# An attention stage whose inverse goes through memory: L is sent out before its diagonal is set, and four steps change their place

## The chip, the cores and the metric

One Trainium2 chip, one core of it. The metric is the device time of one execution in microseconds (us). TensorE does matmuls and 128x128 transposes, DVE is VectorE, ACT is ScalarE, POOL is GpSimd, SP is SyncE, which here only issues DMAs.

## The reference, cut to what matters

The program runs four layers on x of 32 x 256 tokens of 128 features, each with a layer norm before it and a residual after it: attention, feed-forward, a state-space layer, feed-forward. The change is in attention, a gated delta rule:

```
q, k, v = x@Wq+bq, x@Wk+bk, x@Wv+bv
k = k / max(norm(k), 1e-12)
alpha, beta, gate = sigmoid(x@Wa+ba), sigmoid(x@Wb+bb), sigmoid(x@Wg+bg)
for each token t:                      # S is 128 x 128 for each of the 32 sequences
    S = S @ (alpha_t * (I - beta_t * k_t k_t^T)) + beta_t * v_t k_t^T
    o_t = (q_t @ S) * gate_t
y = o @ Wo + bo
```

## The kernel before, in words

The kernel computes attention in blocks of 128 tokens ("tiles"). Four tiles, two whole sequences, are a group; there are 16 groups. In a tile the sequential rule becomes a triangular system: with L the matrix of gated products of keys (unit diagonal), the kernel needs the inverse of L and applies it to v. A sequence is two tiles, so the second tile's v is first corrected by what the first tile wrote.

The inverse is built bottom up. Its 16x16 diagonal blocks ("leaves", eight in a tile, 32 in a group) are brought to 32 partitions by writing L to memory (`LT_dram`) and reading back only the leaves (`leafV`). GpSimd eliminates them in 14 pairs of small operations (`leaf_steps`, L571 and L575), DVE makes 2I - V of them (`leafR`, L1136), and they go out (`R_dram`) and back as a block-diagonal matrix `Rm`. From there the levels 16, 32 and 64 are joined on TensorE (`times_M`, `times_T`), with transposes by DVE and copies by ACT between them.

The order of the work is written out by hand. `in_order` calls, on each engine, `attention_half` (on SP `leaves_half`) for h = 0 to 18, with up to four groups in flight: b = group h (k projection, norm of k, decay, L), s = h - 1 (leaves), i = h - 2 (v, the rest of the inverse, q, gate), e = h - 3 (applying the inverse, outputs), and nxt, whose layer norm is being made. Every engine runs its instructions in the order of the code; semaphores join the engines. `wait_ge(X, done(n))` waits until X has been done for group n.

What each engine does in a half, as far as the change and the working speak of it:
- TensorE: k (L1560), w0 (L1568: inverse times v for the first tile of each of the two sequences), v (L1575), spread alpha (L1582), correction (L1591), Z4 (L1542), WT (L1603: for all four tiles v transposed times R), T4 (L1549), transposes of k (L1613), PT (L1621), Z5 (L1542), G (L1634), transposes of x (L1536), O (L1645, L1647), T5 (L1549), q (L1656), Z6, y (L1666), gate (L1671), R6.
- DVE: bias of k (L1071), shift of the layer norm (L1028), `Tm` by transposing `Rm` (L1081), bias of v (L1084), sum of k's squares (L1089) and its maximum with 1e-24 (L1091), v's correction (L1096), the mask of level 16 (L1046), normalised k (L1106), scans (L1112), the gate on PT and later on L (L1056, twice), leafR (L1136), og = O times gate (L1143), transposes of level 32 (L1149), the residual (L1155).
- GpSimd: bias onto x (L584), rstd of the layer norm (L555, L558), leaf steps 1 to 3, 1/norm of k (`kinv`, L594), leaf steps 4 to 14, and last the select that sets L's diagonal to one (L600).
- ACT: sigmoid, copies out of PSUM, k's squares (L785).
- SP: R's leaves out (L496), L out (L500), R in (L506), L's leaves in (L511). A wait of SP is recorded one line above the issue that stands behind it.

Of the kernel before, what the change touches and what calls it, by code (L numbers as in the profile page):

```python
# [75 lines left out]
def build(nc, x_in, Wq, bq, Wk, bk, Wv, bv, Wa, ba, Wb, bb, Wg, bg, Wo, bo,  # L76
# [7 lines left out]
    with ctx:  # L84
# [208 lines left out]
        LEAF_STEPS = 2 * (LEAF - 2)  # L293
# [5 lines left out]
        def done(n):  # L299

            return n + STREAMS + 1
# [126 lines left out]
        def _(sp):  # L428
# [62 lines left out]
            def leaves_half(b, s, i, e, nxt):  # L491

                if s is not None:
                    n, k = s
                    sp.wait_ge(leaf_done, done(n))
                    sp.dma_start(dram_leaves(R_dram[k % 2]), leaf_grid(leafR[k % 2][:, :])).then_inc(R_out, 16)  # L496
                if b is not None:
                    n, k = b
                    sp.wait_ge(LT_done, done(n))
                    sp.dma_start(dram_tiles(LT_dram[k % 2]), tile4(LT[k][:, 0:GROUP])).then_inc(LT_out, 16)  # L500
# [6 lines left out]
                if b is not None:  # L507
                    n, k = b
                    sp.wait_ge(LT_out, landed(n))
                    sp.wait_ge(leaf_done, done(n - 2))  # L510
                    sp.dma_start(leaf_grid(leafV[k % 2][:, :]), dram_leaves(LT_dram[k % 2])).then_inc(leaf_in, 16)  # L511
# [33 lines left out]
        def _(pool):  # L545
# [14 lines left out]
            def leaf_steps(n, k, first, last):  # L560

                V = leaf_grid(leafV[k % 2][:, :])
                for s in range(first, last):
                    below = LEAF - 1 - s
                    prod = leaf_tmp[:, 0:s * below].rearrange("r (c t) -> r c t", t=below)
                    at = LEAF_STEPS * n + 2 * (s - 1)
                    if s == 1:
                        pool.wait_ge(leaf_in, landed(n))
                    if at > 0:
                        pool.wait_ge(leaf_step, at)  # L570
# [7 lines left out]
            def attention_half(b, s, i, e, nxt):  # L578

                if e is not None:  # L580
# [16 lines left out]
                if b is not None:  # L597
                    n, k = b
                    pool.wait_ge(LTraw_done, done(n))
                    nc.gpsimd.affine_select(out=tile4(LT[k][:, 0:GROUP]), in_=tile4(LT[k][:, 0:GROUP]),  # L600
                                            compare_op=ALU.not_equal, fill=1.0, base=0,
                                            pattern=[[0, GROUP_TILES], [-1, P]], channel_multiplier=1).then_inc(LT_done, 1)
# [406 lines left out]
        def _(dve):  # L1009
# [51 lines left out]
            def attention_half(b, s, i, e, nxt):  # L1061
# [15 lines left out]
                if i is not None:  # L1077
# [4 lines left out]
                    dve.wait_ge(v_mm, done(n))  # L1082
                    dve.wait_ge(WT_mm, done(n - 2))
                    nc.vector.tensor_tensor(tile4(vtok[k % 2]), tile4(begin_bank[2][:, :]), per_tile(bv_row[:, :]),  # L1084
                                            ALU.add).then_inc(v_done, 1)
                if b is not None:
# [4 lines left out]
                    nc.vector.tensor_scalar(kss[k % 2], kss[k % 2], 1e-24, None, ALU.max).then_inc(kmax_done, 1)  # L1091
                if e is not None:
# [894 lines left out]
```

## Time and profile before

| | us |
|---|---|
| median of 3 runs | 880.91 (879.55 to 883.13) |
| the profiled execution | 879.69 |
| its span, first to last instruction | 877.9 |
| TensorE busy, share of the span | 773.3, 88% |
| DVE busy | 621.8, 71% |
| GpSimd busy | 561.6, 64% |
| ACT busy | 535.7, 61% |

The span is what the traces divide; the time lies 1.8 us above it. Busy time is no bound by itself: an engine that is 88% busy over the span may be filled in one stage and wait in another. The attention stage ends at about 346 us; the rest of the span belongs to the three later layers.

### The profile page before, as it was taken

The page shows a single profiled execution, that of the slowest core. Times are in us where ns is not written, and L with a number is a line of the kernel's source. Part 1 is how long each engine was busy: PE and PEld are TensorE (multiplying, and loading weights), DVE is VectorE, ACT ScalarE, POOL GpSimd, SP SyncE. Part 2 cuts the span into 40 slices and gives each one's busy share as a digit, 9 for nine tenths or more (in the row PEclk, how much of TensorE's full clock was granted, in tenths as well). Part 3 has the DMA queues.
Part 4 walks back from the last instruction along what each step waited for, and adds up shares of the span by engine and source line. Part 5 has one row for each costly group of instructions (what it writes and reads, how often), then busy time and mean ns, then how long its engine had stood idle before and what let it go on. Part 6 is the DMA issues. An engine that isn't in the chain of part 4 may idle for free. (4 is left out here: it accounts for less than half of the span.)

```text
span 877.9 us, 16088 instructions
## 1 busy us (share of the span) xinstructions
PE 773.3 (88%) x5146; PEld 551.7 (63%) x5146; DVE 621.8 (71%) x1739; ACT 535.7 (61%) x1035; POOL 561.6 (64%) x901
## 2 busy tenths in 40 slices
PE   1369999999999895999856999999999999959997
PEld 1258888888888774666634456656555555545665
DVE  1357878777878753888664678888887777637885
ACT  2224443443345323888644878978887788828986
POOL 1267567666766620788711579778868876757785
PEclk9979999999999999999955899999999999979999
DMA  7511111111111100000000000000000000000112
GB/s 195 134 28 37 46 28 28 38 46 28 28 42 41 29 14 1 1 1 0 2 0 8 1 1 3 7 1 2 9 0 1 7 4 1 1 0 25 48 49 73
DMA packets 59420, 22.16 MB, mean 25 GB/s; under 512 B 22224, under 2 KB 59088, under 8 KB 59344
## 3 DMA queue, kind: packets, MB, share of 16 engines
q1 hardware_dynamic: 59344, 21.23, 9.5%
q8 instruction: 37, 0.61, 0.3%
q14 instruction: 39, 0.32, 0.1%
HBM read 11.59 MB, written 9.63 MB: 24 GB/s over the span
## 5 line engine op out<-in xcount | busy, mean ns | idle before, releaser
L1405 DVE SCALAR_TENSOR_TENSOR arena<-bank,convw_sb,arena 128x510 f32<-128x510 f32 (+2 forms) x192 | 142.4, 744 | 42.2 <-ACT arena L898 37.5
L667 POOL TENSOR_TENSOR arena<-arena 128x768 f32<-128x768 f32 x64 | 114.9, 1815 | 12.8 <-ACT arena L925 10.9
L641 POOL TENSOR_TENSOR arena<-ff,arena 128x512 f16<-128x512 f32 x64 | 73.6, 1159 | 23.0 <-ACT arena L867 21.0
L571 POOL TENSOR_TENSOR leaf_tmp<-leafV 32x14 f32<-32x14 f32 (+6 forms) x224 | 55.8, 249 | 37.1 <-DMA leafV<-LT_dram 21.8
L862 ACT ACTIVATE ff<-bank 128x512 f32<-128x512 f32 x96 | 56.2, 586 | 32.2 <-PE bank L1708 32.0
L770 ACT ACTIVATE ff<-bank 128x256 f32<-128x256 f32 (+2 forms) x80 | 33.9, 424 | 65.1 <-PE bank L1549 37.7
L575 POOL TENSOR_TENSOR leafV<-leafV,leaf_tmp 32x14 f32<-32x14 f32 (+6 forms) x224 | 62.3, 278 | 17.6
L1795 PE MATMUL bank<-xnT,win_sb 128*128 128x512 f32 x128 | 71.8, 645 | 0.0
L1221 DVE SCALAR_TENSOR_TENSOR ff<-bank,ff 128x512 f32<-128x512 f32 x96 | 64.6, 684 | 8.9 <-ACT ff L862 8.0
L919 ACT ACTIVATE arena<-bank 128x384 f32<-128x384 f32 x128 | 59.8, 492 | 15.5 <-PE bank L1810 15.3
L755 ACT ACTIVATE xnT<-bank 128x512 f32<-128x512 f32 x34 | 20.3, 596 | 79.1 <-PE bank L1536 79.0
L763 ACT ACTIVATE xn<-x_all,shift,rstd 128x128 f32<-128x128 f32 x136 | 55.6, 480 | 18.8 <-DVE shift L1028 18.8
L555 POOL TENSOR_TENSOR var_eps<-mv,eps_cols 128x4 f32<-128x4 f32 x34 | 7.1, 210 | 93.0 <-DVE mv L1021 93.0
L1056 DVE SCALAR_TENSOR_TENSOR arena<-bank,arena 128x256 f32<-128x256 f32 (+1 forms) x128 | 44.6, 411 | 24.1 <-PE bank L1621 16.2
L673 POOL TENSOR_TENSOR arena<-arena 128x512 f32<-128x512 f32 x32 | 40.1, 1268 | 29.8 <-DVE arena L1412 29.4
L898 ACT ACTIVATE arena<-bank,convb_sb,convw_sb 128x512 f32<-128x512 f32 x64 | 49.9, 781 | 11.9 <-PE bank L1795 11.9
L1821 PE MATMUL bank<-arena 128*64 128x256 f32 (+1 forms) x512 | 48.4, 332 | 3.5 <-DVE x_all L1277 2.6
L1536 PE MATMUL bank<-tab,xn 128*128 128x128 f32 x136 | 24.0, 306 | 28.5 <-issue 16.5
L1821 PEld LDWEIGHTS bank<-arena 128*64 128x64 f32 x512 | 31.9, 136 | 25.7 <-issue 11.7
L1707 PE MATMUL bank<-xh,gate 128*128 128x512 f16 x96 | 37.7, 393 | 8.6 <-DVE xl L1206 7.9
L1808 PE MATMUL bank<-ff 12*128 12x384 f16 x128 | 43.1, 337 | 2.3 <-ACT arena L919 2.3
L1808 PEld LDWEIGHTS bank<-ff 12*128 12x128 f16 x128 | 11.6, 91 | 52.4 <-issue 25.1
(199 smaller groups left out, 2239.2 us busy)
## 6 DMA issues: line engine op xcount, KB each, us to landing
LT_dram<-arena SPq DMA_DIRECT2D x16, 256.0 KB, 2.4
ff<-R_dram SPq DMA_DIRECT2D x16, 256.0 KB, 3.0
out<-x_all SPq DMA_DIRECT2D x8, 512.0 KB, 3.2
x_all<-in_L_attn_a_x SPq DMA_DIRECT2D x7, 512.0 KB, 7.3
ff<-pieces_dram SPq DMA_DIRECT2D x48, 6.0 KB
x_all<-in_L_attn_a_x SPq DMA_DIRECT2D x2, 256.0 KB, 3.6
R_dram<-tab SPq DMA_DIRECT2D x2, 256.0 KB, 2.7
leafV<-LT_dram SPq DMA_DIRECT2D x16, 32.0 KB, 2.7
```

Of the source, the lines that this page charges most:

```text
L571: nc.gpsimd.tensor_tensor(prod, V[:, s:s + 1, s + 1:LEAF].broadcast_to([leaf_rows, s, below]), V[:, 0:s, s:s + 1].broadcast_to([leaf_rows, ...
L575: nc.gpsimd.tensor_tensor(V[:, 0:s, s + 1:LEAF], V[:, 0:s, s + 1:LEAF], prod, ALU.subtract).then_inc(leaf_step, 1)
L641: nc.gpsimd.tensor_tensor(of_block(hl[u], j), hidT[u][:, j, :], of_block(hh[u], j), ALU.subtract).then_inc(hl_done[u], 1)
L667: nc.gpsimd.tensor_tensor(score[h], cb[g % 2], hgam[h], ALU.mult).then_inc(score_done, 1)
L763: last = nc.scalar.activation(xn[u][:, cols(t)], x_all[:, n % GROUPS * GROUP + t * P:n % GROUPS * GROUP + (t + 1) * P], ACT.Identity, scal ...
L862: nc.scalar.activation(silu_g[u][:, j, :], bank[u][(1, 3, 1)[j]][:, :], ACT.Silu, scale=DEQUANT).then_inc(silu_done[u], 1)
L919: nc.scalar.activation(hgam[h][:, batch * TRI:(batch + 1) * TRI], step_bank[batch][:, 0:TRI], ACT.Exp).then_inc(hgam_done, 1)
L1221: nc.vector.scalar_tensor_tensor(hidT[u][:, j, :], bank[u][(2, 0, 2)[j]][:, :], DEQUANT, silu_g[u][:, j, :], ALU.mult, ALU.mult).then_inc( ...
L1405: nc.vector.scalar_tensor_tensor(acc_of[:, :, s:SEQ], src_of[:, :, 0:SEQ - s], convw_sb[:, r, TAPS - 1 - s:TAPS - s], acc_of[:, :, s:SEQ], ...
L1795: mm(conv_bank[r % 2][:, :], win_sb[:, INNER + r * P:INNER + (r + 1) * P], xnT[b % XNT_SETS][:, :], start=True, stop=True).then_inc(conv_m ...
L1808: mm(to[:, 0:TRI], from_rows[side][rows, at * P:(at + 1) * P], to_rows[side][rows, at * TRI:(at + 1) * TRI], start=True, stop=False)
L1821: last = mm(y_bank[r][k * HEAD_DIM:(k + 1) * HEAD_DIM, batch * SEQ + c * P:(batch + 1) * SEQ], x_of[:, 2 * batch + c, h * HEAD_DIM:(h + 1) ...
```

## The change

- L is written to memory as soon as DVE has gated it (`LTraw_done`), with whatever stands on its diagonal. SP issues it first in its half, ahead of R's leaves; the leaves' read comes before R's read.
- The leaves' diagonals are set to one by a memset of `leafV` ahead of the first leaf step; the leaf steps wait for the select as well. A group's leaf work counts 29 steps instead of 28.
- The select on L itself moves from the end of GpSimd's half, for b, to the start of the next one, for the same group (now s). It waits until L's copy out has landed.
- On DVE, the sum of k's squares and the maximum move ahead of v's bias; the two parts of v (bias, correction) now follow one another. og moves ahead of leafR.
- On TensorE, WT of the first tile of each sequence is made by transposing `w0tok` (the same values, since w0 is R transposed times v), before the wait for the corrected v; two tiles of matmuls are left behind that wait.

```diff
-        LEAF_STEPS = 2 * (LEAF - 2)
+        LEAF_STEPS = 2 * (LEAF - 2) + 1
...
+                if b is not None:
+                    n, k = b
+                    sp.wait_ge(LTraw_done, done(n))
+                    sp.dma_start(dram_tiles(LT_dram[k % 2]), tile4(LT[k][:, 0:GROUP])).then_inc(LT_out, 16)
                 if s is not None:
                     n, k = s
                     sp.wait_ge(leaf_done, done(n))
                     sp.dma_start(dram_leaves(R_dram[k % 2]), leaf_grid(leafR[k % 2][:, :])).then_inc(R_out, 16)
                 if b is not None:
                     n, k = b
-                    sp.wait_ge(LT_done, done(n))
-                    sp.dma_start(dram_tiles(LT_dram[k % 2]), tile4(LT[k][:, 0:GROUP])).then_inc(LT_out, 16)
+                    sp.wait_ge(LT_out, landed(n))
+                    sp.wait_ge(leaf_done, done(n - 2))
+                    sp.dma_start(leaf_grid(leafV[k % 2][:, :]), dram_leaves(LT_dram[k % 2])).then_inc(leaf_in, 16)
                 if s is not None:
                     n, k = s
                     sp.wait_ge(WT_mm, done(n - 2))
                     sp.wait_ge(T_done, done(n - 2))
                     sp.wait_ge(R_out, landed(n))
                     sp.dma_start(tile4(Rm[k % 2]), dram_tiles(R_dram[k % 2])).then_inc(R_in, 16)
-                if b is not None:
-                    n, k = b
-                    sp.wait_ge(LT_out, landed(n))
-                    sp.wait_ge(leaf_done, done(n - 2))
-                    sp.dma_start(leaf_grid(leafV[k % 2][:, :]), dram_leaves(LT_dram[k % 2])).then_inc(leaf_in, 16)
...
-                    at = LEAF_STEPS * n + 2 * (s - 1)
+                    at = LEAF_STEPS * n + 2 * (s - 1) + 1
                     if s == 1:
                         pool.wait_ge(leaf_in, landed(n))
-                    if at > 0:
-                        pool.wait_ge(leaf_step, at)
+                        pool.wait_ge(LT_done, done(n))
+                        if n > 0:
+                            pool.wait_ge(leaf_step, at - 1)
+                        nc.gpsimd.memset(leafV[k % 2][:, 0:LEAF * LEAF:LEAF + 1], 1.0).then_inc(leaf_step, 1)
+                    pool.wait_ge(leaf_step, at)
...
+                if s is not None:
+                    n, k = s
+                    pool.wait_ge(LTraw_done, done(n))
+                    pool.wait_ge(LT_out, landed(n))
+                    nc.gpsimd.affine_select(out=tile4(LT[k][:, 0:GROUP]), in_=tile4(LT[k][:, 0:GROUP]),
+                                            compare_op=ALU.not_equal, fill=1.0, base=0,
+                                            pattern=[[0, GROUP_TILES], [-1, P]], channel_multiplier=1).then_inc(LT_done, 1)
                 if e is not None:
...
                 if s is not None:
                     leaf_steps(*s, 4, LEAF - 1)
-                if b is not None:
-                    n, k = b
-                    pool.wait_ge(LTraw_done, done(n))
-                    nc.gpsimd.affine_select(out=tile4(LT[k][:, 0:GROUP]), in_=tile4(LT[k][:, 0:GROUP]),
-                                            compare_op=ALU.not_equal, fill=1.0, base=0,
-                                            pattern=[[0, GROUP_TILES], [-1, P]], channel_multiplier=1).then_inc(LT_done, 1)
...
                     nc.vector.transpose(Tm[k % 2], Rm[k % 2]).then_inc(T_done, 1)
-                    dve.wait_ge(v_mm, done(n))
-                    dve.wait_ge(WT_mm, done(n - 2))
-                    nc.vector.tensor_tensor(tile4(vtok[k % 2]), tile4(begin_bank[2][:, :]), per_tile(bv_row[:, :]),
-                                            ALU.add).then_inc(v_done, 1)
                 if b is not None:
                     n, k = b
                     dve.wait_ge(ksq_done, done(n))
                     nc.vector.tensor_reduce(kss[k % 2], tile4(ksq[k % 2]), AX.X, ALU.add).then_inc(kss_done, 1)
                     dve.wait_ge(kss_done, done(n))
                     nc.vector.tensor_scalar(kss[k % 2], kss[k % 2], 1e-24, None, ALU.max).then_inc(kmax_done, 1)
+                if i is not None:
+                    n, k = i
+                    dve.wait_ge(v_mm, done(n))
+                    dve.wait_ge(WT_mm, done(n - 2))
+                    nc.vector.tensor_tensor(tile4(vtok[k % 2]), tile4(begin_bank[2][:, :]), per_tile(bv_row[:, :]),
+                                            ALU.add).then_inc(v_done, 1)
...
+                if e is not None:
+                    n, k = e
+                    dve.wait_ge(OT_mm, done(n))
+                    dve.wait_ge(g_done, done(n))
+                    dve.wait_ge(y_mm, done(n - 2))
+                    nc.vector.tensor_tensor(og[k % 2], end_bank[2][:, :], gT[k % 2], ALU.mult).then_inc(og_done, 1)
                 if s is not None:
                     n, k = s
                     dve.wait_ge(leaf_step, LEAF_STEPS * (n + 1))
                     V, eye2 = leaf_grid(leafV[k % 2][:, :]), leaf_grid(two_eye)
                     nc.vector.scalar_tensor_tensor(leaf_grid(leafR[k % 2][:, :]), V, -1.0, eye2,
                                                    ALU.mult, ALU.add).then_inc(leaf_done, 1)
-                if e is not None:
-                    n, k = e
-                    dve.wait_ge(OT_mm, done(n))
-                    dve.wait_ge(g_done, done(n))
-                    dve.wait_ge(y_mm, done(n - 2))
-                    nc.vector.tensor_tensor(og[k % 2], end_bank[2][:, :], gT[k % 2], ALU.mult).then_inc(og_done, 1)
...
                     n, k = e
+                    pe.wait_ge(og_done, done(n - 1))
+                    for t in range(BATCHES):
+                        nc.tensor.transpose(end_bank[2][:, cols(2 * t)], w0tok[k % 2][:, cols(t)], ident)
                     pe.wait_ge(v1_done, done(n))
-                    pe.wait_ge(og_done, done(n - 1))
-                    for t in range(GROUP_TILES):
+                    for t in range(1, GROUP_TILES, 2):
                         last = mm(end_bank[2][:, cols(t)], vtok[k % 2][:, cols(t)], Rm[k % 2][:, cols(t)], start=True, stop=True)
                     last.then_inc(WT_mm, 1)
```

## Rows read from the trace of the kernel before

**Rows 1.** Windows: length; busy of PE, PEld, DVE, ACT, POOL; granted clock; DMA.
```profile
71.98:281.01 209.03, 202.74 (x1538) 176.51 (x1537) 163.80 (x475) 89.02 (x194) 138.52 (x395) 1.00 0.15 35
246.87:263.94 17.07, 16.76 (x131) 14.66 (x129) 13.65 (x41) 7.33 (x17) 11.61 (x33) 1.00 0.16 39
```

**Rows 2.** Waits from 60 to 320 us: waiter, releaser, us, times, longest.
```profile
POOL leaf_tmp L571 <- DMA leafV<-LT_dram: 11.4, 11, 2.0
...
SPq L505 <- DMA R_dram<-leafR: 16.4, 15, 2.6
```

**Rows 3.** Timeline of TensorE's matmuls in the quiet half: start, us, operation, count.
```profile
250.09 1.00 PE L1542 MATMUL bank<-ff,arena 128*128 128x64 f32 x8
251.40 1.16 PE L1603 MATMUL bank<-ff,arena 128*128 128x128 f32 x8 [0.31 <-DVE arena L1096]
252.39 1.00 PE L1549 MATMUL bank<-ff 128*128 128x64 f32 x8
253.23 0.60 PE L1613 MATMUL bank<-tab,arena 128*128 128x128 f32 x4
253.67 1.47 PE L1621 MATMUL bank<-arena,ff 128*128 128x256 f32 x8
```

**Rows 4.** Timeline of DVE in the same half.
```profile
248.94 0.70 DVE L1081 STREAM_TRANSPOSE ff<-ff 128x512 f32<-128x512 f32 x1
249.57 0.65 DVE L1084 TENSOR_TENSOR arena<-bank,bv_row 128x512 f32<-128x512 f32 x1
250.15 0.67 DVE L1089 TENSOR_REDUCE arena<-arena 128x4 f32<-128x512 f32 x1
...
250.93 0.41 DVE L1096 TENSOR_TENSOR arena<-arena,bank 128x256 f32<-128x256 f32 x1
...
252.14 0.74 DVE L1106 TENSOR_TENSOR arena<-arena 128x512 f32<-128x512 f32 x1 [0.47 <-POOL arena L594]
...
257.44 1.39 DVE L1056 SCALAR_TENSOR_TENSOR arena<-bank,arena 128x256 f32<-128x256 f32 x4
259.81 0.83 DVE L1136 SCALAR_TENSOR_TENSOR leafR<-leafV,tab 32x256 f32<-32x256 f32 x1 [0.98 <-POOL leafV L575]
```

**Rows 5.** Timeline of ACT in the same half.
```profile
248.99 0.63 ACT L785 ACTIVATE arena<-arena 128x512 f32<-128x512 f32 x1
```

**Rows 6.** Timeline of GpSimd in the same half.
```profile
247.75 1.02 POOL L558 TENSOR_TENSOR rstd<-var_eps,half_neg 128x4 f32<-128x4 f32 x1
249.08 0.20 POOL L571 TENSOR_TENSOR leaf_tmp<-leafV 32x14 f32<-32x14 f32 x1 [0.31 <-DMA leafV<-LT_dram]
...
251.10 1.01 POOL L594 TENSOR_TENSOR arena<-arena,half_neg 128x4 f32<-128x4 f32 x1 [0.28 <-DVE arena L1091]
...
259.74 0.63 POOL L600 TENSOR_SCALAR_AFFINE_SELECT arena<-arena 128x512 f32<-128x512 f32 x1
260.35 1.45 POOL L584 TENSOR_TENSOR arena<-x_all,bo_row 128x512 f32<-128x512 f32 x1
```

**Rows 7.** Timeline of SP's issues in the same half: start of issue, us.
```profile
260.67 0.32 SPq L496 DMA_DIRECT2D R_dram<-leafR  x1
261.04 0.48 SPq L500 DMA_DIRECT2D LT_dram<-arena  x1
262.46 0.38 SPq L506 DMA_DIRECT2D ff<-R_dram  x1
263.46 0.32 SPq L511 DMA_DIRECT2D leafV<-LT_dram  x1
```

**Rows 8.** A memset on GpSimd at the start of the program: ns min/median/max.
```profile
L546 POOL MEMSET half_neg<- x1: 104/104/104, 0.7 to 0.7; 128x8 f32 x1
```

**Rows 9.** Timeline of DVE from 68 to 70 us.
```profile
68.77 0.40 DVE L1136 SCALAR_TENSOR_TENSOR leafR<-leafV,tab 32x256 f32<-32x256 f32 x1
```

**Rows 10.** Timeline of DVE from 57 to 60 us, in the third half.
```profile
57.69 0.71 DVE L1081 STREAM_TRANSPOSE ff<-ff 128x512 f32<-128x512 f32 x1 [2.77 <-DMA ff<-R_dram]
```

**Rows 11.** The page's list of DMA issues: KB each, median us from issue to landing.
```profile
ff<-R_dram SPq DMA_DIRECT2D x16, 256.0 KB, 3.0
```

## The prediction

> **What bounds the kernel now.** I read the windows first, the attention stage as a whole and one half of it, then the waits, then the timelines of one half of the attention stage engine by engine. The change touches the attention stage alone. There the kernel runs nineteen "halves" (16 groups and a lag of 3); a half works on group b at its start, s (select and leaf inverse), i (the rest of the inverse) and e (outputs). Twelve full halves, from the k projection of one at 71.98 us to that of another at 281.01 us, take 209.03 us, and TensorE is busy in 202.74 of them with the full 2.4 GHz granted (1.00); a single quiet half takes 17.07 us with TensorE busy for 16.76 [rows 1]. Twelve quiet ones would be 204.84, so 4.19 us in this stretch are something else than the usual pace.
>
> The usual pace is TensorE's. The one place where it stands in a quiet half is before L1603 (WT = v times R): 0.31 us recorded as idle, for the corrected v of DVE's L1096 [rows 3, 4]. From start to start it is more: L1542's eight matmuls take 0.84 (the spacing of L1549 to L1613, which is the same shape: 252.39 to 253.23), so TensorE could go on at 250.09 + 0.84 = 250.93 and goes on at 251.40, 0.47 lost.
>
> The 4.19 us come from the second loop, which runs over GpSimd and SP: leaf steps end (GpSimd), select L600, leafR on DVE, R out, L out after it, L's leaves back in, leaf steps again. In the quiet half it closes with hardly any slack: leaf steps end just ahead of 259.74, L's copy out is issued at 261.04, the leaves' read at 263.46 [rows 6, 7], and L571 has already waited for such a read 11 times for 11.4 us in all, up to 2.0 [rows 2]. R's own copy out also landed late sometimes: L505 waited 16.4 us over 15 times, a mean of 1.09, but up to 2.6 [rows 2]. When either transfer is late by about one us, the half lasts longer.
>
> **L out without its diagonal.** Now L goes out when DVE's L1056 ends, 257.44 + 1.39 = 258.83 [rows 4], not after leaf steps, select and R's issue at 261.04 [rows 7]: 2.2 us earlier. Its leaves are then read 2.42 us after its issue (261.04 to 263.46), as now, so the whole L to leaf path starts 2.2 us earlier. GpSimd does not gain that: it first must do rstd, whose 1.02 us end at 248.77, and the first leaf step begins at 249.08 [rows 6], so 0.31 is what it can gain. A memset of the leaf diagonals is added there. Nearest row: a memset of 128x8 takes 0.104 [rows 8]; with the 0.08 that a dependent GpSimd operation follows behind its predecessor's end, 0.18; the upper bound is the start-to-start step of a leaf operation, 0.28 (1.74, below, over six), the lower 0.10. With 0.18 the steps start at 248.98 at the latest, about 0.1 earlier than now, and the price is covered. After three pairs of steps (249.08 to 251.10, less about 0.28 idle, 1.74) GpSimd is ready for kinv at 250.72.
>
> **Select at the head of the half.** L600 (0.63) leaves the end of the leaf steps and moves to where GpSimd sat waiting for mv. It waits for L's landing, 258.5 + 2.42 = 260.9 (the times from here on already have the 0.4 us of the sum taken off), so it ends at 261.6, and the bias add of 1.45 behind it ends at 263.0; rstd of the next half starts at 247.75 [rows 6] + 17.07 - 0.4 = 264.4, with a small addition of 0.3 ahead of it, so GpSimd is wanted at 264.1. Slack 1.1 us. Queued behind this wait are the bias add, rstd and all leaf steps; DVE's shift, and with it the whole chain to v, waits for rstd. Cost nothing while L lands within 3.5 us of its issue.
>
> **leafR.** It took 0.83 while select ran on GpSimd (259.74) [rows 4, 6], and 0.40 when GpSimd was not selecting [rows 9]. Now select has not begun, so I take 0.40. The Trainium skill says of this ("SBUF — State Buffer", who interferes with whom) that a vector instruction with two SBUF inputs and a GpSimd one that reads SBUF exclude each other for the whole instruction; the two rows agree. With the steps' end at 259.4 (kinv is 0.38 earlier, see below), leafR ends at 259.85 and R goes out at 259.9, not 260.67; R in follows 1.79 later (260.67 to 262.46 [rows 7]) at 261.7 and, landing 3.0 after its issue [rows 11], is there at 264.7. DVE wants it at 248.94 + 17.07 - 0.4 = 265.6 [rows 4]: slack 0.9, where it was 0.55. SP's order changes too: the leaves' read now stands ahead of R in. It is issued at 260.9, before R in may be, and delays it by nothing. og ahead of leafR: og needs the O matmuls only and uses DVE's 0.98 us idle before leafR [rows 4]; its consumer L1666 stands behind q and Z6 on TensorE, so this is worth nothing in a quiet half, and something in those where the leaf steps end late.
>
> **Squares of k ahead of v's bias and correction.** DVE runs T (L1081), bias add (L1084), reduce (L1089), max, correction (L1096). With the reduce moved up, it would start at 249.57, where the bias add starts; but the squares end on ScalarE at 248.99 + 0.63 = 249.62 [rows 5], 249.65 with the semaphore. So the corrected v comes 0.08 later, the rest of the sum being the same operations. Reduce and max take 0.78 up to the next operation (250.15 to 250.93 [rows 4]), so kmax comes at about 249.65 + 0.8 = 250.5; GpSimd is ready at 250.72, kinv starts then, 0.38 earlier than 251.10 [rows 6]. kn follows 1.04 later at 251.76 instead of 252.14 and ends at 252.5 [rows 4]; the transposes of kn on TensorE (253.23, or 252.8 after the gain below) never wait for it: cover 0.3 us, which a memset of 0.28 would still leave at 0.2.
>
> **Two transposes ahead of the corrected v.** For the even tiles WT is the transpose of w0, which is in SBUF already. Four transposes take 0.44 from start to start (L1613, 253.23 to 253.67), eight instructions of four matmuls 0.99 (L1603 to L1549) [rows 3]. So 0.50 of matmuls leave the path behind the wait and 0.22 of transposes go into the 0.47 of the wait. New start of T4: 251.40 + 0.08 + 0.50 = 251.98 instead of 252.39, a gain of 0.41; if the first pair pays its start alone (half of the 0.99 is then 0.55), 0.36. I take 0.40. Everything behind it (T4, kT, PT, Z5, G, O, T5, q, Z6, y, g, R6) runs without a gap on TensorE and moves up by it, since the waits there (copies on ScalarE, gates on DVE) all follow from TensorE's own results.
> The Trainium skill ("TensorE: Matmul & The Clock Gate", Part 4: PE-mode transpose) says that transposes do not count as busy for the clock as matmuls do. That speaks against trading matmuls for transposes. The twelve halves had twelve transposes each (L1582, L1613, L1536) and were granted 1.00 throughout [rows 1]; two more in each is what is new.
>
> **The sum.** Thirteen full halves (the twelve and the next) by 0.40: 5.2. Of the 4.19 us of late transfers, those of the leaves' read vanish (landed by 263.4, wanted at 265.4 when rstd ends: 2 us of slack); a late R can still cost, with 0.9 of slack: I leave 1.0, so 3.2 gained. The last three halves: the last one has no other group's work between the steps of its one group, so TensorE waits for v there and half of the 0.99 is saved, the other two save some 0.28 each: 1.0. The first halves: T of the first inverse waited 2.77 us for R's read behind L's copy out, until 57.69 [rows 10]; L now leaves before it, and I take that wait to be about 0.9 shorter, against 0.3 for a select and memset that stand ahead of the first kinv: 0.6. Total 10.0 us. The profiled execution took 879.69 with a span of 877.9, so 869.7 in its like; the median of the three runs is 880.91, which gives 870.9. I say 871.0. What follows the stage (both feed-forward stages and the state-space stage) is untouched.
>
> **Rivals.** About 4.4 us, half a per cent, is what a measurement can tell from none.
> *The forecast*, 60 in 100: 868 to 873.
> *Late transfers stay or find another victim* (R out and R in instead of the leaves), 18 in 100: the gain is 5.2 + 1.0 + 0.6, so 874. For it: the longest wait of L505 was 2.6 against a mean of 1.09, more than the slack of 0.9. Against it: most of the late ones were the leaves'.
> *TensorE packs wholly*, 7 in 100: if v came early enough to hide the wait, a half would lose 0.47 + 0.28 = 0.75, 13 of them 9.8, and the time would be 866. Against it: nothing in v's chain gets shorter.
> *Nothing comes of it*, 8 in 100: squares later than thought (a slip of 0.5 instead of 0.08 eats the transposes' gain) and the late transfers stay: 879.
> *Slower*, 5 in 100: select waits for L's landing at the head of GpSimd's queue. It decides from a landing 3.5 us after issue; to be 4.4 us slower than now it must be 14.4 / 13 = 1.1 us beyond that in each half, 4.6 us after issue, where 2.42 is seen: 886.
> *The clock gate*, 2 in 100: TensorE is busy for 16.76 us of a half at 2.4 GHz [rows 1]; one half wholly at 1.2 GHz would cost up to 16 us and bring 887. By the skill's rule this could follow from the transposes; the granted 1.00 speaks against it.
> The range 866 to 876 leaves out the last three cases and a little more. Faster by over half a per cent 0.85, within 0.09, slower 0.06.
>
> **What the profile after would show.** From one k projection to the next 16.7 us in quiet halves. Two transposes of w0 start right behind Z4, and TensorE's wait for v stands between them and four matmuls. No wait of the leaf product for its read; leafR at 0.40, og before it. kinv 0.4 us earlier against T. The forecast is wrong if the wait for v grows beyond 0.25, if T waits for R's read, or if var_eps waits for GpSimd itself.

## The result, and the profile after

The changed kernel takes 868.59 us, median of four executions (867.31 to 870.12), against 880.62 for the kernel before on the same chip: a ratio of 0.9865, with a 95% interval from 0.9835 to 0.9894. The profiled execution took 869.76 with a span of 868.0, 9.9 less than before's 877.9. (Ratios and their intervals here and below are worked out from the single executions, so a ratio can differ a little from the quotient of two medians.)

The windows answer to [rows 1]: the same twelve halves, and one quiet half.

```profile
71.18:272.84 201.66, 198.84 (x1514) 172.30 (x1513) 158.49 (x475) 89.14 (x194) 139.74 (x410) 1.00 0.15 37
239.31:256.07 16.76, 16.55 (x128) 14.36 (x126) 13.22 (x41) 7.33 (x17) 11.53 (x34) 1.00 0.15 38
```

The twelve take 7.37 us less. A quiet half takes 16.76 instead of 17.07, and eleven of the twelve are quiet (before: five within 0.06 of the quiet length, the others up to 18.33). The columns are those of [rows 1]; the granted clock, 1.00, is unchanged.

TensorE in a quiet half, from its timeline (start, us, operation, count, idle before):

```profile
242.53 1.00 PE L1548 MATMUL bank<-ff,arena 128*128 128x64 f32 x8
243.37 0.39 PE L1608 MATMUL bank<-tab,arena 128*128 128x128 f32 x2
243.97 0.71 PE L1611 MATMUL bank<-ff,arena 128*128 128x128 f32 x4 [0.21 <-DVE arena L1102]
244.52 1.00 PE L1555 MATMUL bank<-ff 128*128 128x64 f32 x8
245.36 0.61 PE L1621 MATMUL bank<-tab,arena 128*128 128x128 f32 x4
```

The two transposes (L1608) stand where TensorE stood idle in [rows 3]. Two tiles of matmuls are left behind the wait for v (L1611), and T4 (L1555) follows 0.55 after they start, not 0.99.

DVE in the same half (it answers to [rows 4]):

```profile
241.39 0.70 DVE L1085 STREAM_TRANSPOSE ff<-ff 128x512 f32<-128x512 f32 x1
242.10 0.69 DVE L1089 TENSOR_REDUCE arena<-arena 128x4 f32<-128x512 f32 x1
242.82 0.17 DVE L1091 TENSOR_SCALAR arena<-arena 128x4 f32<-128x4 f32 x1
242.90 0.69 DVE L1096 TENSOR_TENSOR arena<-bank,bv_row 128x512 f32<-128x512 f32 x1
243.51 0.41 DVE L1102 TENSOR_TENSOR arena<-arena,bank 128x256 f32<-128x256 f32 x1
243.84 0.42 DVE L1050 TENSOR_TENSOR ff<-bank,tab 128x256 f32<-128x256 f32 x1
244.17 0.68 DVE L1112 TENSOR_TENSOR arena<-arena 128x512 f32<-128x512 f32 x1
...
247.32 1.39 DVE L1060 SCALAR_TENSOR_TENSOR arena<-bank,arena 128x256 f32<-128x256 f32 x4 [0.66 <-PE bank L1629]
...
251.27 0.69 DVE L1143 TENSOR_TENSOR arena<-bank,arena 128x512 f32<-128x512 f32 x1 [0.30 <-PE bank L1655]
251.88 0.40 DVE L1148 SCALAR_TENSOR_TENSOR leafR<-leafV,tab 32x256 f32<-32x256 f32 x1
```

From T to v's correction are 2.12 us (241.39 to 243.51), where before they were 1.99: the reduce starts 0.08 later than DVE could, as worked out, and 0.05 more goes into the order of the rest. Normalised k (L1112) starts without a wait. leafR takes 0.40.

GpSimd and SP around the end of the half (they answer to [rows 6, 7]):

```profile
243.07 1.01 POOL L604 TENSOR_TENSOR arena<-arena,half_neg 128x4 f32<-128x4 f32 x1
...
253.48 0.64 POOL L587 TENSOR_SCALAR_AFFINE_SELECT arena<-arena 128x512 f32<-128x512 f32 x1 [1.72 <-DMA LT_dram<-arena]
254.09 1.28 POOL L594 TENSOR_TENSOR arena<-x_all,bo_row 128x512 f32<-128x512 f32 x1
256.68 0.20 POOL L555 TENSOR_TENSOR var_eps<-mv,eps_cols 128x4 f32<-128x4 f32 x1 [1.32 <-DVE mv L1025]
```

SP's instructions, from the timeline of its queue:

```profile
251.00 0.38 SPq L496 DMA_DIRECT2D LT_dram<-arena  x1
252.31 0.32 SPq L500 DMA_DIRECT2D R_dram<-leafR  x1
253.30 0.32 SPq L505 DMA_DIRECT2D leafV<-LT_dram  x1
254.09 0.38 SPq L511 DMA_DIRECT2D ff<-R_dram  x1
```

L goes out first, select waits for it on an engine that has nothing else to do, and after the bias add GpSimd is still idle for 1.3 us before var_eps: this is the slack that the prediction put at 1.1. No leaf product and no var_eps waits for a DMA in any quiet half. The leaves' read, which now stands ahead of R's, also takes less itself: a median of 1.9 us from issue to landing, where it was 2.7.

Where the 9.9 us went, from the starts of the k projection and of the residual add in both traces: the first three halves 0.80, the twelve full halves 7.37, from there to the thirteenth residual add 0.33, and the last three halves took 0.65 more than before (49.60 against 48.95). The stage ends 7.85 us earlier. From the start of the last residual add to the end of the span 530.15 us pass, where they were 532.2, 2.05 less in this pair of executions. The code there is the same, and in the twelve other profiles below this part takes 529.2 to 535.8 us, so these 2 us are not put down to the change.

### The profile page after: what moved, and what is told of

It is laid out like the page before. It is cut to its first block and busy times, and to the rows that moved or that the text cites. A ratio compares the mean times of both kernels' runs of the same rounds, so it can differ in the third digit from the quotient of the medians.

```text
span 868.0 us, 16041 instructions
## 1 busy us (share of the span) xinstructions
PE 769.9 (89%) x5114; PEld 549.0 (63%) x5114; DVE 614.7 (71%) x1739; ACT 535.9 (62%) x1035; POOL 560.6 (65%) x917
```

## The experiments

All are made from the kernel before or from the changed kernel. The length of a quiet half is read from one k projection to the next. A ratio compares with the kernel before on the same chip; its median there was 882.74 us for the path of L, the two transposes and the two orders on DVE, 880.79 for v's bias, the reductions, both and the changed kernel again, and 881.23 for the rest. The expectations start from 880.9 or 868.6.

**The path of L alone.** The kernel before with the changes on SP and GpSimd, without those on DVE and TensorE; the read of the leaves is issued ahead of that of R, too.

```diff
@@ leaves_half, SP @@
+                if b is not None:
+                    n, k = b
+                    sp.wait_ge(LTraw_done, done(n))
+                    sp.dma_start(dram_tiles(LT_dram[k % 2]), tile4(LT[k][:, 0:GROUP])).then_inc(LT_out, 16)
                 if s is not None:
...
@@ leaf_steps, GpSimd @@
+                        nc.gpsimd.memset(leafV[k % 2][:, 0:LEAF * LEAF:LEAF + 1], 1.0).then_inc(leaf_step, 1)
...
@@ attention_half, GpSimd @@
+                if s is not None:
+                    n, k = s
+                    pool.wait_ge(LTraw_done, done(n))
+                    pool.wait_ge(LT_out, landed(n))
+                    nc.gpsimd.affine_select(out=tile4(LT[k][:, 0:GROUP]), in_=tile4(LT[k][:, 0:GROUP]),
...
```

> The kernel before with the path of L alone (L out before its diagonal, select at the head of GpSimd's half, memset of the leaves' diagonals, SP's order); DVE's order and TensorE's four tiles of WT matmuls are those of before. Theory (two loops): the quiet half stays at 17.07 us, since TensorE's wait for v is untouched, and the longer halves (17.3 to 18.3) vanish, so about 3.7 us from these, 0.7 from the first halves: 876. Rival (the path of L is hidden anyway, the gain of the changed kernel is all TensorE's): 880 to 881, with halves of 17.6 still there.

Measured: ratio 0.9948 (0.992 to 0.9976), median 878.16: 4.6 us gained, about what had been expected. The quiet half is 17.07, as it should be. No leaf product waits for its read in a full half any more. But four of the twelve halves are long (17.93, 17.61, 17.53, 18.5), not none. The profiled execution, 885.46 us, is the longest of the twelve executions, so it does not stand for all. In each of the four halves DVE's T waits for the read of R, in the longest like this:

```profile
196.23 0.71 DVE L1085 STREAM_TRANSPOSE ff<-ff 128x512 f32<-128x512 f32 x1 [1.33 <-DMA ff<-R_dram]
```

and the list of DMAs of the window 189 to 193 us shows what was under way:

```profile
q8 instruction: 1, 0.02, 2.2%
q14 instruction: 1, 0.01, 0.8%
issues: line engine op xcount, KB each, median us to landing
ff<-R_dram SPq DMA_DIRECT2D x1, 256.0 KB, 3.4
R_dram<-leafR SPq DMA_DIRECT2D x1, 32.0 KB, 3.6
leafV<-LT_dram SPq DMA_DIRECT2D x1, 32.0 KB, 2.9
```

R's leaves out took 3.6 us instead of the usual 1.7, in a window in which the instruction queues loaded two pieces. In the halves of 17.61 and 17.53 the copy out took 1.7, but R's read 4.45 and 4.41 instead of 2.8. The path of L is worth something alone (half a per cent), for the leaves; it does not keep R from being late, so the expectation's "the longer halves vanish" was too much.

**The two transposes alone**, made in the kernel before.

```diff
@@ attention_half, TensorE @@
+                    pe.wait_ge(og_done, done(n - 1))
+                    for t in range(BATCHES):
+                        nc.tensor.transpose(end_bank[2][:, cols(2 * t)], w0tok[k % 2][:, cols(t)], ident)
                     pe.wait_ge(v1_done, done(n))
-                    pe.wait_ge(og_done, done(n - 1))
-                    for t in range(GROUP_TILES):
+                    for t in range(1, GROUP_TILES, 2):
```

> The kernel before with the two transposes of w0 in WT alone. Theory (two loops): TensorE alone could do a half in 17.07 - 0.44 = 16.63, but the loop of leaf steps, select, L out and leaves in takes 17.07 less its 0.28 us idle at kinv, 16.8, and now has no slack against a late transfer: quiet halves of 16.8 at best, late ones as long as before, 877 to 879. Rival (the parts add up): 13 halves by 0.44 and 0.8 at the end, 874.

Measured: ratio 0.9986 (0.9953 to 1.0019), median 881.22: no difference that can be told, and by the medians 1.5 us gained where 2 to 4 had been expected. TensorE's side works, T4 starts 0.55 after L1605; and what was gained is lost three lines on, at the transposes of k, which wait for DVE's normalised k:

```profile
93.98 0.71 PE L1605 MATMUL bank<-ff,arena 128*128 128x128 f32 x4
94.53 1.00 PE L1549 MATMUL bank<-ff 128*128 128x64 f32 x8
96.03 0.66 PE L1615 MATMUL bank<-tab,arena 128*128 128x128 f32 x4 [0.50 <-DVE arena L1106]
```

Behind this stands GpSimd, whose leaf steps began late:

```profile
92.49 0.20 POOL L571 TENSOR_TENSOR leaf_tmp<-leafV 32x14 f32<-32x14 f32 x1 [1.13 <-DMA leafV<-LT_dram]
```

The halves of this execution (884.95 us, above the median) are 17.0 to 17.7, and one 20.06, in which T waits 1.70 for R. In ten of the twelve the leaf product waits over 0.8 us for its read. The second loop, over leaves and memory, has become the bound. The theory of two loops holds, more strongly than expected: it gave 16.8 for the best halves, and only 16.98 was seen.

**Everything but the transposes**: the diff above, the other way round, in the changed kernel.

```diff
@@ attention_half, TensorE @@
-                    for t in range(BATCHES):
-                        nc.tensor.transpose(end_bank[2][:, cols(2 * t)], w0tok[k % 2][:, cols(t)], ident)
                     pe.wait_ge(v1_done, done(n))
-                    for t in range(1, GROUP_TILES, 2):
+                    pe.wait_ge(og_done, done(n - 1))
+                    for t in range(GROUP_TILES):
```

> The changed kernel with the WT of all four tiles by matmuls behind the corrected v, as before. Theory: the 0.44 us of two tiles of matmuls come back on the path behind v, which is 0.13 later than in the kernel before, so a quiet half takes 17.2 us, 0.44 more than 16.76, thirteen of them 5.7 and 0.8 at the end: 875. Rival (the transposes only fill a wait that another releaser ends anyway, the gain is the earlier L): 16.8 to 16.9, 870.

Measured: ratio 0.9959 (0.9931 to 0.9987), median 877.95; the quiet half is 17.20, as expected:

```profile
248.52 1.00 PE L1548 MATMUL bank<-ff,arena 128*128 128x64 f32 x8
249.96 1.16 PE L1609 MATMUL bank<-ff,arena 128*128 128x128 f32 x8 [0.43 <-DVE arena L1102]
250.95 1.00 PE L1555 MATMUL bank<-ff 128*128 128x64 f32 x8
```

0.44 us a half are the transposes', 0.13 of them pay for the later v. The time is 3 us above the expected 875. In the profiled execution 1.7 us of it are two halves (18.2 and 17.93) in which T waits 1.03 and 0.76 for R. So the transposes alone give 0.1%, which is not told from nothing, the rest without them 0.4%, both together 1.35%: the two parts give more together than the sum of what each gives alone.

**The two orders on DVE put back**, each alone in the changed kernel. First v's bias (L1096) back ahead of the squares of k:

```diff
                     nc.vector.transpose(Tm[k % 2], Rm[k % 2]).then_inc(T_done, 1)
+                    dve.wait_ge(v_mm, done(n))
+                    dve.wait_ge(WT_mm, done(n - 2))
+                    nc.vector.tensor_tensor(tile4(vtok[k % 2]), tile4(begin_bank[2][:, :]), per_tile(bv_row[:, :]),
+                                            ALU.add).then_inc(v_done, 1)
                 if b is not None:
```

Then leafR (L1148) back ahead of og:

```diff
                     gated(LT_strip, LT[k], k, begin_bank).then_inc(LTraw_done, 1)
-                if e is not None:
-                    n, k = e
-                    dve.wait_ge(OT_mm, done(n))
-                    dve.wait_ge(g_done, done(n))
-                    dve.wait_ge(y_mm, done(n - 2))
-                    nc.vector.tensor_tensor(og[k % 2], end_bank[2][:, :], gT[k % 2], ALU.mult).then_inc(og_done, 1)
                 if s is not None:
...
```

> The changed kernel with v's bias ahead of k's squares again. Theory: v is corrected 0.13 us earlier, but kinv starts 0.45 later and the transposes of k then wait some 0.07 for kn, so a half of 16.70 instead of 16.76 and 0.8 us less in all: within 1.5 us of the changed kernel's 868.6. Rival (the squares' place is what lets kn and TensorE be in time): kinv 0.4 later costs 0.3 us or more a half, 873 or above.

> The changed kernel with og behind leafR again. Theory: og ends by 252.97 where TensorE asks for it at 253.52, leafR and R out come 0.1 us earlier, nothing else moves: 868.6, the half 16.76. Rival (og's place is part of the gain): y waits, half longer by 0.2 or more, 871.

Measured: 0.9885 (0.9837 to 0.9932) with the squares back, 0.9881 (0.9835 to 0.9926) with og back; the changed kernel's 0.986 lies in both intervals. The quiet half is 16.83 with the squares back and 16.76 with og back. In the first, what the earlier v gives is taken by the transposes of k, which wait for kn at 245.42 (0.15 behind the end of T4's eight): the order is worth 0.07 us a half, where 0.06 the other way had been expected. og's place is worth nothing in a quiet half, as expected; the times, 875.13 and 873.62 in the median, are too scattered to say more. The single executions of both spread from 868 to 876 us. The profiled one with the squares back shows one reason. Its last half took 18.36 us, that of the changed kernel 14.22. The windows of both follow, first with the squares back (length, busy shares as above, then the granted clock):

```profile
324.90:343.50 18.60, 13.47 (x60) 10.28 (x58) 3.65 (x10) 6.58 (x13) 0.00 (x0) 0.67 0.00 0
```

The changed kernel's:

```profile
323.60:337.90 14.30, 9.13 (x58) 6.87 (x57) 3.69 (x10) 6.58 (x13) 0.00 (x0) 1.00 0.00 1
```

In one the granted clock is 0.67 on average, in the other 1.00, with the same work. TensorE stands idle there six times between short pieces, since one group alone is left.

**v's bias out of v's way.** The bias add is for group i, the correction behind it for group e. Nothing ties them, so the add goes behind the scans, ahead of the gate on PT.

```diff
                     nc.vector.tensor_scalar(kss[k % 2], kss[k % 2], 1e-24, None, ALU.max).then_inc(kmax_done, 1)
-                if i is not None:
-                    n, k = i
-                    dve.wait_ge(v_mm, done(n))
-                    dve.wait_ge(WT_mm, done(n - 2))
-                    nc.vector.tensor_tensor(tile4(vtok[k % 2]), tile4(begin_bank[2][:, :]), per_tile(bv_row[:, :]),
-                                            ALU.add).then_inc(v_done, 1)
...
                     last.then_inc(gam_done, 1)
+                if i is not None:
+                    n, k = i
+                    dve.wait_ge(v_mm, done(n))
+                    dve.wait_ge(WT_mm, done(n - 2))
+                    nc.vector.tensor_tensor(tile4(vtok[k % 2]), tile4(begin_bank[2][:, :]), per_tile(bv_row[:, :]),
+                                            ALU.add).then_inc(v_done, 1)
```

> The changed kernel with v's bias (0.69 us on DVE) moved from in front of the correction to behind the scans, where DVE is idle for 0.66 us; the bias is for another group than the correction. Theory (v's chain on DVE is the last limit): the corrected v is there 0.6 us earlier, ahead of the end of the two transposes, TensorE packs, a half takes about 16.4 (16.76 less the 0.38 from 243.59 to 243.97), thirteen of them 5 us: 864. Rival (the next limit is right behind, kn or T waiting for R's read, or GpSimd): half 16.65 or more, 867 to 868.

Measured: ratio 0.9809 (0.9765 to 0.9853), median 863.02, 5.5 less than the changed kernel on the same chip (868.48). The intervals of the two ratios still overlap a little; the halves tell the difference. Eleven of the twelve halves take 16.39, and TensorE goes from the transposes to the matmuls without a wait:

```profile
240.12 0.39 PE L1608 MATMUL bank<-tab,arena 128*128 128x128 f32 x2
240.34 0.61 PE L1611 MATMUL bank<-ff,arena 128*128 128x128 f32 x4
240.80 1.10 PE L1555 MATMUL bank<-ff 128*128 128x64 f32 x8
```

while DVE does the bias where it was idle before PT's gate:

```profile
239.65 0.41 DVE L1096 TENSOR_TENSOR arena<-arena,bank 128x256 f32<-128x256 f32 x1
...
243.34 0.66 DVE L1120 TENSOR_TENSOR arena<-bank,bv_row 128x512 f32<-128x512 f32 x1
243.92 1.38 DVE L1060 SCALAR_TENSOR_TENSOR arena<-bank,arena 128x256 f32<-128x256 f32 x4
```

v's chain on DVE was the last limit of the changed kernel's half. At 16.39 TensorE is busy for the whole of it.

**The reductions of the weights one half later.**

```diff
-                if h == GROUPS:
+                if h == GROUPS + 1:
                     all_weights = ff_raw[:, :, :].rearrange("p k h -> p (k h)")
```

> The changed kernel with the two reductions over the feed-forward weights (2.7 us on DVE) one half later. In their half TensorE waits 2.92 us for T, and its clock is then granted at 0.6 to 0.7 for some 7 us. Theory (the 1.4 us that this half became longer with the change are the clock after that wait): the wait shrinks to about 0.5, the clock stays at the higher level, and the half loses 2.5 to 5 us: 864 to 866. Rival (that half is bound by leaf steps or R's copy): under 1 us, 868.

Measured: ratio 0.9838 (0.9797 to 0.9879), median 866.6, which by the intervals is not told from the changed kernel; the profile tells it. The half takes 15.17, TensorE's wait for T is 0.19 instead of 2.92, and the clock of the first 15 us is granted in full. In the changed kernel's first profile this half took 21.06 with 0.77 granted; in its repetition on this chip, below, 17.88 with 1.00. So 2.7 us are the wait's; the other 3.2 of the 21.06 went with the clock, and they were gone in the repetition without this edit. The windows, first with the reductions late:

```profile
290.00:305.00 15.00, 13.69 (x103) 11.54 (x102) 8.95 (x25) 6.04 (x13) 10.14 (x33) 1.00 0.08 20
```

The changed kernel's:

```profile
289.50:304.50 15.00, 10.97 (x62) 10.15 (x61) 7.49 (x23) 3.60 (x9) 9.29 (x32) 0.77 0.03 8
```

Part of it is given back in the two halves behind (15.13 and 15.58 against 14.32 and 14.22). The reductions, which now stand in the first of them, are hardly the reason: behind them T still waits 0.32 for R's read, and the repetition below, with the reductions in their old place, has 15.01 and 15.58. In the last half the eight matmuls of PT (L1629) took 2.93 us instead of 1.57, with 0.89 granted over the half.

**Both.**

The two diffs above together, in the changed kernel.

> Both of the two before. Theory: they touch different halves and add up, 860 to 861. Rival: one eats the other, 864.

Measured: ratio 0.9777 (0.9735 to 0.9819), median 859.83 (857.67 to 866.0), 8.6 less than the changed kernel on the same chip. The two gains add up, as expected, and this version beats both kernels.

**The changed kernel again**, as the base of that chip.

> The changed kernel itself, for a base on the same chip: 868.6, halves of 16.76 us.

Measured: 868.48 (867.15 to 870.25), ratio 0.986 (0.9824 to 0.9896). Ten of the twelve halves take 16.76, the first 17.31 and the last 17.32. In the last, T waits for R, whose read took 4.7 us instead of 2.8:

```profile
257.92 0.71 DVE L1085 STREAM_TRANSPOSE ff<-ff 128x512 f32<-128x512 f32 x1 [0.60 <-DMA ff<-R_dram]
```

The half with the weights' reductions took 17.88 us here, with the same wait of 2.9 and the clock granted at 1.00 behind it; the last two took 15.01 and 15.58. So the 21.06 of the first execution are not in the code. Of the twelve profiles with the reductions in this place, two have 17.9 in this half and ten have 19.4 to 22.0.

**The price and the cover of the memset**: 3 more of them, and in the second kernel 8, on a tile that nothing reads.

```diff
+        spare = sb("spare", [leaf_rows, 8 * LEAF])
...
+                        for more in range(3):
+                            nc.gpsimd.memset(spare[:, more * LEAF:(more + 1) * LEAF], 1.0)
                         nc.gpsimd.memset(leafV[k % 2][:, 0:LEAF * LEAF:LEAF + 1], 1.0).then_inc(leaf_step, 1)
```

> The changed kernel with three memsets of 32x16 more (into a spare tile) ahead of the leaves' own, 0.12 us each by its trace. Theory: kinv comes 0.28 to 0.36 later, kn ends 0.5 ahead of TensorE's need for it, so the half stays at 16.76. Rival (GpSimd bounds the half as well): the half grows by the 0.36.

> The same with eight more memsets, some 0.9 us. Theory: kinv 0.85 later is 0.3 to 0.4 more than the cover of 0.5, so the half grows to 17.1 or 17.2: this is the point from which a memset would have cost. Rival (nothing waits for kinv that long): 16.76.

Measured, one execution each: 867.89 and 872.39 us, the quiet half 16.76 and 16.75. The longer time of the second is not in its quiet halves; its last half took 18.32, the one with the reductions 20.89. Eight memsets that nothing waits for took 0.42 us together, not 0.9:

```profile
240.51 0.42 POOL L574 MEMSET spare<- 32x16 f32 x8
240.87 0.12 POOL L575 MEMSET leafV<- 32x16 f32 x1
```

DVE at normalised k in the same half:

```profile
243.80 0.75 DVE L1115 TENSOR_TENSOR arena<-arena 128x512 f32<-128x512 f32 x1 [0.22 <-POOL arena L607]
```

DVE now waits 0.22 for kinv, and TensorE does not notice. The memset costs nothing, and 0.36 more would not either; where the cover ends was not reached.

**SP's order**: the read of R ahead of the read of the leaves again.

```diff
-                if b is not None:
-                    n, k = b
-                    sp.wait_ge(LT_out, landed(n))
-                    sp.wait_ge(leaf_done, done(n - 2))
-                    sp.dma_start(leaf_grid(leafV[k % 2][:, :]), dram_leaves(LT_dram[k % 2])).then_inc(leaf_in, 16)
                 if s is not None:
...
                     sp.dma_start(tile4(Rm[k % 2]), dram_tiles(R_dram[k % 2])).then_inc(R_in, 16)
+                if b is not None:
+                    n, k = b
+                    sp.wait_ge(LT_out, landed(n))
+                    sp.wait_ge(leaf_done, done(n - 2))
+                    sp.dma_start(leaf_grid(leafV[k % 2][:, :]), dram_leaves(LT_dram[k % 2])).then_inc(leaf_in, 16)
```

> The changed kernel with SP issuing the read of R ahead of the read of the leaves, as before. Theory (a late R is the work of packets of the instruction queues on one DMA ring, wherever SP's order stands): halves of 16.76, R asked for 1.79 us behind its own copy out, leaves 0.9 later and still in time, at most the odd late half. Rival (the leaves' read in front delays R): T no longer waits at all and the odd long halves are gone; or the leaves are late and the half is over 16.9 throughout.

Measured, one execution: 871.14 us. The halves are 16.76 but for the first and one of 17.83, in which GpSimd's memset waited 1.44 us for the leaves and TensorE 0.87 at the transposes of k. The read of the leaves is issued 0.46 behind that of R (239.10 and 239.56), 3.6 us after L's copy out instead of 2.3, and takes a median of 2.6 us instead of 1.9; in the long half it took 4.4. With SP's old order the leaves can be late again; SP's order is part of what keeps them off the path. One half in one execution shows how it can go, not how often.

## Why the prediction was right

**TensorE's wait for v is the pace of a quiet half: right, the size 0.31 instead of 0.40.** Of the terms, the two matmul tiles take 0.55 behind the wait, the prediction's upper bound (0.46 where v's bias is late and there is no wait, 240.34 to 240.80); v comes 0.13 later, not 0.08. With both, 0.44 - 0.13 = 0.31, and without the transposes the half is 0.44 longer. Twelve halves give 3.7.

**The leaves' read as the cause of long halves, and their end: right in the main, but not the whole of the 4.19 us.** The twelve halves had 4.19 us beyond the quiet length, now 0.52, so 3.67 are gained, where 3.2 had been taken. Of the 4.19, 2.4 stood in six longer halves in which the leaf product, and not T, waited for its read. The other 1.8 stood in two, of 17.63 and 18.33, in which T waited for R as well (0.47 and 1.16) and the wait of TensorE followed T's. The longer, in the kernel before:

```profile
214.79 0.71 DVE L1081 STREAM_TRANSPOSE ff<-ff 128x512 f32<-128x512 f32 x1 [1.16 <-DMA ff<-R_dram]
```

The leaves' share is gone: no full half of the path of L alone, or of the changed kernel, has such a wait. R's share is not. The profiled execution of the changed kernel had no late R in the twelve halves, which is luck: its repetition had one (0.57 us), the path of L alone 3.3 us of long halves, in all four of which T waited for R, and og put back one half of 20.29 us, in which T waited 1.92 for R and the granted clock was then 0.75 over 5 us. In the quiet half R's read is issued at 254.09 and takes 2.8, and T wants it at 258.15: a slack of 1.2, where 0.9 had been worked out, and at times too short. The rival "late transfers find another victim" therefore lives on in single executions, and the prediction's own sign of being wrong, a T that waits for R's read, appeared in the repetition.

**The select at the head of GpSimd's queue: right in the quiet halves, and not in the first full half.** The slack is 1.3 against 1.1. In the first full half L's copy out lands late for GpSimd, the bias add behind it ends late, and shift waits for rstd. The copy itself takes the usual 2.4 us; it is issued late, 3.1 us ahead of the k projection instead of 5.1. Timelines of the changed kernel, GpSimd, then DVE:

```profile
70.62 0.64 POOL L587 TENSOR_SCALAR_AFFINE_SELECT arena<-arena 128x512 f32<-128x512 f32 x1 [4.09 <-DMA LT_dram<-arena]
```

```profile
73.81 0.17 DVE L1032 SCALAR_TENSOR_TENSOR shift<-mv,rstd 128x4 f32<-128x4 f32 x1 [0.54 <-POOL rstd L558]
```

This half takes 17.28. It is the slower rival's queue behind select, without the slow landing of 4.6 us that the rival asked for, and it costs 0.5 us in one half of the twelve. It is no accident of one execution: of the twelve profiles with select in this place, eleven have a wait of shift for rstd in the first full half, of 0.16 to 0.60.

**leafR at 0.40 and kinv without a wait: right.** leafR no longer meets select. kinv starts 1.68 after T where it started 2.16 after it (0.48 earlier, 0.38 had been worked out), and DVE's 0.47 us before normalised k are gone.

**The clock: no loss in the stage.** 14 transposes a half, two of them in place of matmuls, and 1.00 granted in the twelve halves. The Trainium skill's rule ("TensorE: Matmul & The Clock Gate", Part 4: PE-mode transpose) would have let one expect a lower clock; no run here shows one in a full half without a wait of over a microsecond ahead of it. Of the 168 full halves in the fourteen profiles two were granted less than 1.00, those of 20.06 us (0.91) and 20.29 us (0.92), in which TensorE first waited 1.24 and 1.46 for T.

**The last halves: wrong.** The step "the last three: 1.0" failed. The last two are 0.25 and 0.45 shorter, as worked out; the third from the end is 1.35 longer. TensorE waits 2.9 us in it, before as after, and how long the clock stays low behind that wait differs between executions: 19.71 before, 21.06 after, 17.88 in the repetition. The prediction took the clock of the trace of before as given.

**The sum: near, and in part by luck.** The stage gained 7.85 in the profiled pair where 10.0 had been worked out: 0.80 in the first halves (0.6 forecast), 4.1 by TensorE's wait in thirteen halves (5.2), 3.65 in late transfers (3.2), and -0.65 in the last three (1.0). In the repetition the stage ends 9.3 us earlier than before, so over half of what was missing lies within the scatter of single executions. The median moved by 12.0, to 868.59, 2.4 below the forecast. The 2 us of the pair behind the stage are unexplained, and so is the rest up to 12. A late R that lowers the clock, and the last halves' clock, move single executions by 3 to 4 us each, which bounds what one pair of profiles can say about a sum.

## What to carry to other kernels

Where two engines' loops take nearly the same time a round, price a change by both: shortening either alone gave 0.1% (not told from nothing) and 0.4% here, both together 1.35%. A write that must wait for a small correction of its data can go out without it, if the correction can be made again where the data is read back. And look at what stands ahead of the last operand in an in-order queue: moving an add for another group, 0.7 us long, out of the way was worth 0.37 us a half, as much again as the change's own 0.31.

## What the runs showed of the hardware that had not been expected

- A 16 KB piece of the instruction queue went out about once a half, and an 8 KB one as often. In the fourteen traces, from 60 to 285 us, ten of the 184 copies out of R's leaves had one that started within 1.2 us of their issue: they took 1.9 to 3.7 us. Nine had one that started later: 1.7. None of the 165 others took over 2.4. Of 180 of R's reads, 2.8 to 2.9 us as a rule, 25 had a 16 KB piece that was under way at their issue or started within 1.8 us of it: they took 3.4 to 4.9. Of the 155 others two took over 3.5 (4.2 and 4.8). So a piece early in a transfer and a late landing fall together; that the piece causes the delay is still an inference, no run here took the pieces away.
- TensorE's clock after the same 2.9 us of idle: granted 0.77 over 15 us in one execution, 1.00 in another of the same program. The last half, with six short waits, was granted 1.00, 0.89 or 0.67 in different executions (14.2, 15.6 and 18.4 us), worth up to 4 us.
- Memsets of 32x16 on GpSimd that nothing waits for follow one another in 0.05 us; the one that the next operation waits for takes 0.12, and 0.20 to that operation's start.
